# Preparing the delta stage's inputs inside the first stage, and a gate whose token part is computed once for all heads

## The reference, cut to what matters

```python
q = silu(conv(hs @ Wq)); k = silu(conv(hs @ Wk)); v = silu(conv(hs @ Wv))   # 4 heads of 64
beta = sigmoid(hs @ Wb)                                  # one per token and head
# delta rule, chunks of 32 tokens, per head
q = l2norm(q); k = l2norm(k); v = v * beta; kb = k * beta
A = where(strictly_lower, kb @ k.T, 0)                   # 32 x 32
inv = solve_triangular(eye + A, eye)                     # 32 x 32
u = inv @ v; w = inv @ kb
def step(S, (qi, ki, ui, wi)):                           # scan over 32 chunks
    attn = where(lower, qi @ ki.T, 0)
    u_i = ui - wi @ S
    return S + ki.T @ u_i, qi @ S + attn @ u_i
# gate: per token AND head, on [hs (256), 16 statistics of that head]
hgate = gelu(concat([hs_broadcast_over_heads, stats]) @ mlp_w1 + mlp_b1)     # 256 hidden
logits = hgate @ mlp_w2 + mlp_b2
o = mix of short FIR, long FIR, delta_out, v by softmax(logits); rms norm; @ Wo
```

## Time and profile before

| what | us |
|---|---|
| median of 3 runs | 5963.18 (5955.74 to 5968.25) |
| span of the profiled execution | 5957.4 |
| first stage | 0 to about 2707 |
| filter stage | to 3002.91 |
| inverse stage | 3002.91 to 3604.29 |
| delta stage | 3604.29 to about 5822 |
| last stage | to the end |

### The profile page before, as it was taken

One profiled execution on the slowest core, in us unless ns is written; L12 is line 12 of the kernel. 1 busy time (PEld: TensorE's weight loads), 2 busy tenths in 40 slices (PEclk: granted clock), 3 DMA queues, 4 the chain that ended last, 5 costly groups with the idle time before them and its releaser, 6 DMA issues. The chain is left out here.

```text
span 5957.4 us, 119901 instructions
## 1 busy us (share of the span) xinstructions
PE 5355.5 (90%) x42776; PEld 4244.1 (71%) x42776; DVE 4264.6 (72%) x13841; ACT 2668.3 (45%) x6214; POOL 2612.1 (44%) x3780
## 2 busy tenths in 40 slices
PE   6999999999999999988966636999999999999987
PEld 5888888888888888867944424777777777777755
DVE  4777777777777777762238875888888888888871
ACT  2555555555555555542133322444444444444441
POOL 1222222222222222222277742666666666666660
PEclk8999999999999999998955556999999999999998
DMA  1011011011011011006755542222222222222211
GB/s 41 28 36 37 29 35 36 29 34 37 29 35 36 29 35 36 29 29 134 190 149 141 141 108 57 61 62 62 62 61 62 61 60 59 60 62 61 62 35 45
DMA packets 599702, 357.50 MB, mean 60 GB/s; under 512 B 336400, under 2 KB 589136, under 8 KB 599120
## 3 DMA queue, kind: packets, MB, share of 16 engines
q1 hardware_dynamic: 528656, 314.18, 18.9%
q10 hardware_dynamic: 65664, 16.78, 1.2%
q0 software_dynamic: 4800, 18.88, 1.1%
HBM read 212.59 MB, written 137.10 MB: 59 GB/s over the span
## 5 line engine op out<-in xcount | busy, mean ns | idle before, releaser
L526 POOL TENSOR_TENSOR a_shift<-a_mean_var,a_eps 128x2 f32<-128x2 f32 x256 | 71.3, 279 | 1834.9 <-DVE a_mean_var L736 1834.9
L2136 PE MATMUL c_bank<-c_xT,c_gate 128*128 128x512 f32 x1024 | 503.0, 614 | 0.7 <-ACT c_statsT L1889 0.7
L750 DVE SCALAR_TENSOR_TENSOR a_cv<-a_raw,a_taps,a_cv 128x256 f32<-128x256 f32 x1152 | 461.9, 479 | 19.5 <-ACT a_cv L628 10.0
L820 PE MATMUL a_bank<-a_w,a_hidden 128*128 128x256 f32 x2048 | 459.1, 382 | 0.9 <-ACT a_hidden L613 0.9
L918 PE MATMUL a_bank<-a_turned,a_w 128*128 128x256 f32 x2048 | 453.0, 379 | 1.1 <-ACT a_turned L574 1.1
L820 PEld LDWEIGHTS a_bank<-a_w,a_hidden 128*128 128x128 f32 x2048 | 383.8, 190 | 71.8 <-issue 20.6
L918 PEld LDWEIGHTS a_bank<-a_turned,a_w 128*128 128x128 f32 x2048 | 384.1, 190 | 51.2 <-ACT a_turned L574 1.6
L1786 POOL TENSOR_TENSOR c_expd<-c_e,c_logit 128x16 f32<-128x16 f32 x128 | 371.7, 2904 | 50.7 <-DVE c_logit L1972 37.9
L1772 POOL TENSOR_TENSOR c_stats<-c_l2sq,half 128x16 f32<-128x16 f32 x128 | 373.4, 2917 | 15.1 <-DVE c_l2sq L1961 15.1
L2140 PEld LDWEIGHTS c_bank<-c_statsT,c_gate_stats 128*128 128x128 f32 x2048 | 270.0, 192 | 124.9 <-issue 124.9
L1356 POOL TENSOR_TENSOR i_coef<-i_base,i_exponent 128x12 f32<-128x12 f32 x128 | 298.9, 2335 | 71.6 <-issue 52.8
(11 more groups left out here) (295 smaller groups left out, 14140.7 us busy)
## 6 DMA issues: line engine op xcount, KB each, us to landing
a_x<-in_x SPq DMA_DIRECT2D x64, 256.0 KB, 3.3
scratch_xb<-a_xb SPq DMA_DIRECT2D x64, 256.0 KB, 2.1
scratch_q<-a_qkv_rows SPq DMA_DIRECT2D x64, 256.0 KB, 2.2
scratch_k<-a_qkv_rows SPq DMA_DIRECT2D x64, 256.0 KB, 2.7
scratch_v<-a_qkv_rows SPq DMA_DIRECT2D x64, 256.0 KB, 3.0
b_window<-scratch_v SPq DMA_DIRECT2D x8, 2048.0 KB, 22.1
scratch_long<-b_out ACTq DMA_DIRECT2D x8, 2048.0 KB, 24.4
scratch_short<-b_out POOLq DMA_DIRECT2D x8, 2048.0 KB, 18.0
```

The costliest lines, as they stand in the source:

```text
L750: ins = dve.scalar_tensor_tensor(cv[s][:, n, c], raw[s][:, n, c, j:j + TOK], taps[:, n, c, j:j + 1], cv[s][:, n, c], ALU.mult, ALU.add)
L820: ins = pe.matmul(dst[:, t * D:(t + 1) * D], src[s][:, c, tile_cols(t)], weight[:, c], start=(c == 0), stop=(c == chunks - 1))
L2136: pe.matmul(dst[:].rearrange("p (h t) -> p h t", h=H), gate1[:, c, cols], xT[sl][:, c:c + 1].broadcast_to([P, H, P]), start=(c == 0), stop ...
```

## The change

**First stage.** `phase_i` goes; its work becomes parts of `phase_a`'s two-tile step: `beta` (four products of four columns), `squares` (ACT 128x1024, sums on DVE), `powers` (POOL; the sigmoid is made with powers too, and POOL scales the keys), `kT` (four turns, one ACT copy of 128x512), `gram` (32 products), `keep` (two DVE masks). Once a batch `gather` brings one set of 128 triangles back (two transfers of 512 KB), and its inverse by columns is cut in 16 pieces, four a step, on DVE, each instruction linked to the one before. SiLU is also applied to the feature-major q, so q is stored turned. Stored are xb, v, scaled keys, coefficients, grams, and the turns of xb, q and keys: 13 SP transfers a step. `phik_rows`, `phiq_own`, `v_own`, `resid` and `xa` go from two buffers to one, with waits for the last reader of the step before. Shares and depth are new, and so is the order: on PE qkv1, beta, xdT, kT, gram, den, phikT, ffn, x1nT, dS, rdenT, mlp1, scores0, xnT, mlp2, qkvT, scores1, xbT, attn, qkv, wo; before it was qkv, wo, xdT, qkv1, den, phikT, ffn, x1nT, dS, rdenT, mlp1, xnT, scores0, mlp2, scores1, qkvT, xbT, attn.

**Delta stage.** `keys`, `turn_x` and `turn_qk` go; the turned xb, q, keys and the scaled keys are loaded (seven loads a step for five). The gate's token part is one part `base`: four products of 128x128 into one bank. ACT copies it into two held banks, once for each head (`seed`), `pre` adds the statistics with eight products of half height (64 rows), and Gelu reads the held banks; the bias is a row of ones in the statistics. Six banks are left for the others. On PE the order is logits, carry3, solve0, oT, solve3, carry1, Wo, o, dS, solve1, base, carry2, statsT, pre, gram, kS, solve2; before it was pre, solve2, kS, logits, carry3, solve0, oT, solve3, carry1, Wo, turn_x, o, dS, solve1, turn_qk, statsT, carry2, gram. DVE's order is the same but for `carry2`, now ahead of the second norm's statistics.

```diff
@@ phase_a
-    DEPTH = 4.779
+    PERIOD = 10.437
-              ("lnB_stats", 1.69), ("lnB", 1.72), ("xbT", 3.97), ("qkv1", 3.91), ("conv", 1.64), ("qkvT", 0.01)]
+              ("lnB_stats", 2.29), ("lnB", 4.0), ("xbT", 1.39), ("qkv1", 0.11), ("beta", 4.14), ("conv", 1.31),
+              ("qkvT", 1.43), ("squares", 2.59), ("powers", 1.48), ("kT", 0.02), ("gram", 1.54), ("keep", 2.06),
+              ("gather", 33.88), ("inverse0", 2.71), ("inverse1", 2.74), ("inverse2", 2.76), ("inverse3", 0.01)]
-    order = pipelined(shares, STEPS, DEPTH)
+    order = pipelined(shares, STEPS, sum(share for _, share in shares) / PERIOD)
...
+            def powers(i, s):
+                pool.wait_ge(S["ssq_ready"], seq(i, s))
+                in_sbuf(pool, i, s, "beta")
...
+                link(pool.tensor_tensor(beta, e_base[:], beta, ALU.pow))
+                link(pool.tensor_tensor(beta, beta, one_base[:], ALU.add))
+                link(pool.tensor_tensor(coef[s][:], base[s][:], powers_half[:], ALU.pow))
...
+            def invert(piece):
...
+                    for j in columns_of[m]:
...
+                        link(dve.tensor_tensor(part, A_[:, j:j + 1, below_j].broadcast_to(shape),
+                                               T_[:, 0:j, j:j + 1].broadcast_to(shape), ALU.mult))
...
+                        ins = dve.tensor_tensor(rest, rest, part, ALU.add)
+                        if j < CUT - 2:
+                            link(ins)
...
+            def turn_keys(i, s):
+                dst = open_bank(i, s, "kT")
+                pe.wait_ge(S["kn_ready"], seq(i, s))
...
+            def gram(i, s):
+                dst = [open_bank(i, s, "G0", "kT"), open_bank(i, s, "G1")]
@@ phase_c
-    DEPTH = 6.969
+    DEPTH = 6.8950
-    LOADS = 5 * 16
+    LOADS = 7 * 16
+    PRE = [BANKS - C + m for m in range(C)]
+            def seed(i, s):
+                src_ = full(act, i, s, "base")
...
+            def gate_base(i, s):
+                dst = open_bank(i, s, "base")
+                for m in range(C):
+                    cols = slice(m * P, (m + 1) * P)
+                    for c in range(C):
+                        ins = pe.matmul(dst[:, cols], gate1[:, c, cols], xT[s % SLOTS][:, c], start=(c == 0),
+                                        stop=(c == C - 1))
             def gate(i, s):
+                pe.wait_ge(N["pre_seeded"], C * seq(i, s))
                 for m in range(C):
-                    for c in range(C):
-                        pe.matmul(dst[:].rearrange("p (h t) -> p h t", h=H), gate1[:, c, cols],
-                                  xT[sl][:, c:c + 1].broadcast_to([P, H, P]), start=(c == 0), stop=False,
-                                  skip_group_check=True)
+                    for n in range(2):
+                        for g in range(PAIRS):
+                            rows = slice(g * DH, (g + 1) * DH)
+                            ins = pe.matmul(psum[PRE[g]][:, at:at + P], gate1_stats[rows, 2 * g + n, m * P:(m + 1) * P],
+                                            statsT[sl][rows, :], start=False, stop=True, skip_group_check=True)
@@ build
-        phase_i(nc, w, k, scratch, batches, banks)
```

More of the change, by code:

```diff
@@ L30 @@
 BANKS = 8
+CUT = 32
 def pipelined(shares, steps, depth):
@@ L94, with __init__ @@
 class PsumPlan:
-    def __init__(self, order, jobs_of, base, iterations):
+    def __init__(self, order, jobs_of, base, iterations, held=()):
         self.base, self.iterations = base, iterations
+        shared = [b for b in range(BANKS) if b not in held]
         jobs = [(stage, s, late, job) for stage, s, late in order for job in jobs_of.get(stage, ())]
@@ L508, in store_xb, with store_turned @@
                 sp.dma_start(out_v["xb"][i * STEPS + s], xb[s][:]).then_inc(xb_stored[s % OUTS], 16)
[L510 to L515, removed]
+            def store_turned(name, buffer, i, s, stored):
+                for t in range(T):
+                    sp.dma_start(scratch[name][(i * STEPS + s) * T + t], buffer[:, :, tile_cols(t)]).then_inc(stored, 16)
@@ new lines, in store_below, with gather @@
+            def store_below(i, s):
+                alone(sp, S["below_ready"], seq(i, s))
+                for t in range(T):
+                    sp.dma_start(below_v[(i * STEPS + s) * T + t], below[s][:, t]).then_inc(below_stored[s % 2], 16)
+            def gather(i, s):
+                if s < STEPS - 1:
+                    return
+                if i >= 2:
+                    alone(sp, inverse_stored[i % 2], 16 * (i // 2))
+                for m in range(2):
+                    alone(sp, below_stored[m], 16 * T * (STEPS // 2) * (i + 1))
+                for sets in (A_sets, T_sets):
+                    sp.dma_start(sets[i % 2][:].rearrange("p a b -> p (a b)"), sets_v["below"][i])\
+                      .then_inc(sets_in[i % 2], 16)
@@ new lines, in store_inverse @@
+            def store_inverse(i, s):
+                if s == STEPS - 1:
+                    alone(sp, S["inverse_ready"], i + 1)
+                    sp.dma_start(sets_v["inverse"][i], T_sets[i % 2][:].rearrange("p a b -> p (a b)"))\
+                      .then_inc(inverse_stored[i % 2], 16)
+            run(sp, order, batches, {"load": load, "lnB": store_xb, "xbT": store_xbT, "qkvT": store_qv, "kT": store_kn,
+                                     "gram": store_kT,
+                                     "keep": store_below, "gather": gather, f"inverse{PIECES - 1}": store_inverse})
@@ L761, in _ @@
             stages = {
+                "squares": sums, "keep": keep,
                 "ln1_stats": norm_stats(0, x_sb, S["ln1_var"], True),
@@ L1512, in phase_c @@
     FLOOR = 0.08
-    LOADS = 5 * 16
-    shares = [("load", 0.01), ("keys", 5.22), ("load_src", 0.01), ("turn_x", 2.02), ("turn_qk", 2.2), ("gram", 1.78),
-              ("kS", 1.45), ("solve0", 1.36), ("carry1", 2.43), ("solve1", 1.99), ("carry2", 2.69), ("solve2", 0.79),
-              ("carry3", 1.95), ("solve3", 2.34), ("o", 0.01), ("dS", 0.36), ("stats", 8.49), ("l2", 2.7),
-              ("statsT", 2.8), ("pre", 1.26), ("logits", 2.81), ("softmax", 3.03), ("mix", 1.1), ("rms", 4.09),
-              ("oT", 1.69), ("Wo", 1.57), ("lnC_stats", 1.75), ("lnC", 0.01), ("lnD_stats", 3.84), ("lnD", 7.94)]
+    LOADS = 7 * 16
@@ new lines, in phase_c @@
+    shares = [("load", 2.33), ("load_src", 6.66), ("gram", 0.01), ("kS", 1.63), ("solve0", 2.29), ("carry1", 2.47),
+              ("solve1", 1.38), ("carry2", 2.88), ("solve2", 0.58), ("carry3", 1.17), ("solve3", 2.99), ("o", 0.16),
+              ("dS", 0.81), ("stats", 7.9), ("l2", 2.17), ("base", 1.64), ("statsT", 0.2), ("pre", 2.92),
+              ("logits", 2.94), ("softmax", 3.37), ("mix", 0.8), ("rms", 4.03), ("oT", 1.7), ("Wo", 1.34),
+              ("lnC_stats", 2.72), ("lnC", 0.08), ("lnD_stats", 3.84), ("lnD", 7.94)]
```

602 lines of the change are left out of this document (261 added, 341 removed).

## The result

The changed kernel takes 5830.5 us (5826.6 to 5845.3, 4 runs) for 5964.4 us (5955.7 to 5968.3, 4 runs) before: ratio 0.978, 95% interval 0.976 to 0.980. It is faster by 2.2%, where 6200 us was forecast. Its profiled execution spans 5824.8 us, for 5957.4 before, a difference of -132.6.

What follows compares the result with a forecast made beforehand. TensorE was taken to bound the first and delta stages. 5957.4 - 601.4 + 45 + 294 + 499 = 6194 us of span, plus 5.8 for the runs' median, gave 6200; range 5640 to 6420, the forecast's own 5964 to 6417.

Steps and rivals of the forecast that it cites:

- The stage that goes: The inverse stage, which lay alone between the first and delta stages; its removal was forecast at -601.4 us.
- the tail: Behind the first stage: the last batch's grams, store, gather and inverse with nothing to hide them, +45 us (30 to 60).
- the first stage: First-stage step lengthened from 40.0 to 44.6 us by added TensorE work, wait and clock: +4.6 x 64 = +294 us.
- the middle that was taken: In the tail: the inverse of one set alone, 24.5 us, between 16.4 and 32.7.
- 2.0 of work, .9 of wait and 1.7 of clock: First-stage step: TensorE's added products and turns, its wait for the turned keys' copy, and one clock dip, in us.
- covered by TensorE: First stage: VectorE's load of 39.2 us fits in the 44.6 us step, so it was costed at nothing.
- VectorE's loop ahead: Delta stage at full clock: with TensorE's work at 11.8 us, VectorE's loop sets the step, 14.7 to 16.6, taken 16.4.
- a third of the work at full clock: Delta stage: the rest at half clock (22.5 us a step) gives a 20.5 us step, +3.9 x 128 = +499 us.
- The two-thirds rival: Delta stage: clock up for two thirds of the work, step 18.4 us, total 5931 us; chance .23.
- a stretch of the delta stage's filling: The row from 3633 to 3666, clock .50 with TensorE busy 32.26 of 33 us; evidence for a low clock.
- neither is near the bound: Delta stage: ScalarE's two added seeds, about 1 us, and GpSimd's loss of key scaling were costed at nothing.
- The break-even delta step: Delta step of 18.66 us, where its added cost equals the 262 us that the rest gains and the sign turns.

Runs made afterwards that it cites:

- e6_no_inverse: The changed kernel without the columns of the inverse in the first stage, so the delta stage works on a zero inverse; 5686.7 us.
- e11_inverse_moved: The changed kernel with one of four inverse pieces of each first-stage step moved on VectorE to behind the scan; 5755.7 us.
- e8_dense_fill: e7_dense with two more 256-column products on TensorE behind carry3, into a bank that nothing reads; 5657.8 us, ratio .949 to before.
- e14_base_early: The changed kernel with base moved on TensorE from behind solve1 to behind Wo, its two ScalarE seeds with it; 6026.2 us.
- e7_dense: The changed kernel with the gate's token part computed for every head by wide TensorE products into the held banks, without base and seeds; 5744.1 us.
- e1_fill2: The changed kernel with two 512-wide products that nothing reads behind each turn of the statistics in the delta stage; 5865.1 us.
- e9_fill_solves: The changed kernel with two unread 256-column products behind the logits and two behind carry3 in each delta step; 5913.8 us.

## Why the prediction was wrong, point by point

**Right: three of four terms.** The stage that goes, the tail (45 for 45) and the first stage (4.25 for 4.6) came out as worked. The inverse of one set took 22 us (VectorE from 2994.54 to 3016.58), inside 16.4 to 32.7, and below the middle that was taken.

**Right in sum, not in parts: the first stage.** It was 2.0 of work, .9 of wait and 1.7 of clock. Measured: TensorE's busy time grew by 2.8, the work and the slower clock together; at .98, about 4% of 44.25 us is at half clock, .9 us more, not 1.7. TensorE's waits grew by 1.5: .77 for the keys, and 1.6 for VectorE in place of .95 before. VectorE's part the prediction had as "covered by TensorE". e6_no_inverse and e11_inverse_moved show what was wrong there: VectorE's load fits into the step, but inverse pieces stand in its queue ahead of the features and the scan that TensorE needs next. Two misses of opposite sign cancelled.

**Too high: a step at full clock.** TensorE's work was put at 11.8, and the steps at 1.00 have 11.9 to 12.0. But the step was put at 16.4, with VectorE's loop ahead (14.7 to 16.6), and these steps take 15.2 to 15.5. They stand next to slower ones; no run holds this kernel at full clock throughout. That e8_dense_fill takes 16.45 at 1.00 is no confirmation of the 16.4: it has a wider gate and .9 us of filler, and TensorE leads there.

**Wrong: how much of the delta step is at full clock.** That is the step that failed: "a third of the work at full clock gives 16.4/3 + 22.5 x 2/3 = 20.5". The trace's clock of .78 is full clock for 56% of the time. At the measured 15.3 us for a step at full clock that is .56 x 17.86 / 15.3 = .65 of the work, and the other .35 costs .44 x 17.86 / .35 = 22.5, what the prediction had for a step at half clock (its terms were TensorE's work alone; at .54 TensorE is busy 20.4 of 22.2 and waits for the rest). So of the 2.6 us that the forecast was too long, the mix accounts for .32 x 6.1 = 1.9 and the price at full clock for 1.1 x .65 = .7. The two-thirds rival had the mix right: its 18.4 and 5931 us were the nearest case, though it had been given .23.

The premise of the third was that the clock rises once and falls once in each step. The rows at 4509, 4527, 4545 and 4563 show most of a step at one level, and 50 of 111 steps run at 1.00 from end to end. The evidence for the low share was a stretch of the delta stage's filling; but that stretch has no Wo and no output turn in it, and of the gate only 1.2 us at its end; it is the narrow part of a step. It showed that this work doesn't raise the clock. It could not show how much of a whole step is at half clock. Why the full level lasts as long as it does in the changed kernel stays open.

**A slip in the range.** The lower end of the forecast's own range was added up wrong: with 1.7 and 2.9 a step it is 5957.4 - 601.4 + 45 + 110 + 371 + 6 = 5888, not 5964. So by its own terms it reached 1.3% below the time before, and "faster" got too little of its chance. The measured time lies below either.

**Missing: the seeds' queue.** ScalarE's two seeds were costed at nothing, as "neither is near the bound". What counts is who is queued behind them: the copy of the turned statistics, and TensorE waits 1.6 us a step for it. e14_base_early shows that the queue is the reason, and also that the seeds can't simply be moved. Whether the wait costs the step anything in the changed kernel isn't settled; e7_dense, without it, is .7 shorter, but gains clock too.

**The rule that was weighed.** The prediction set the Trainium skill's "TensorE: Matmul & The Clock Gate", section "HAM oscillation — how this bites in real kernels", by which it is gaps that lower the clock, against a row with hardly a gap. The falls shown of e1_fill2 and e9_fill_solves come behind a stretch in which TensorE waits (2.08 busy of 3, 1.25 of 3), in kind as the section has it. But gaps aren't needed for a fall. In the kernel before, the clock falls now and then, and this is one such place, over solves and then Wo:

```profile
4177.20:4180.20 3.00, 2.79 (x36) 1.00 0.58 178
4180.20:4183.20 3.00, 3.00 (x12) 0.50 0.59 152
```

Nor does having no gaps bring the clock back: the row with 32.26 of 33 us busy at .50 and the one from 4527 to 4545, 16.84 busy of 18, stay down. Read as the prediction read it, narrow but not idle, the rule would have kept the step at full clock throughout; the mean was .78.

**The sign.** The break-even delta step was put at 18.66. Measured is 17.86, .8 below, and .8 x 128 = 102 of the 133 us gained; the rest is the first stage's .35 a step, 22, and the delta stage's shorter filling.

## What to carry to other kernels

Work that is taken off the engine that leads is not a gain until one has asked what its clock does without it: here .9 us of useless products in the right place were worth 86 us with the wide gate, while in the changed kernel useless products in one place cost 35 us and in two others 83. Taking a stage's work into the queues of another one is costed by position: for each queue that gets an instruction, name what stands behind it, even where the engine's load leaves room. And a price from a stretch where only part of a step runs says what that part does, not what share of the whole it is.

## What the runs showed of the hardware that was not expected

The granted clock holds its level for about as long as a step, at 1.00 from 4509 to 4524 and at .50 from 4527 to 4545 in a kernel whose steps all do the same; so the same step takes 15.2 or 22.2 us. It can fall over narrow work with hardly a gap, behind 3 us of which TensorE was busy 2.79. And a product that nothing reads, put between narrow pieces of work, can raise the clock of the whole stage: from .91 to 1.00 with two products of 256 columns in a step of 17 us.
